# A two-layer attention and convolution chain fed by one weight stream: patch taps moved ahead of the scores, a projection turned later, middle weights as 8 MB loads, constants split

## What is computed

```
fl = _ln(xf, pn_g, pn_b)                       # 64 patches x 1024
pw = _attn(fl, Wqk_p, PDH)                     # Wqk_p 1024 x 2048
pv = _heads(fl @ Wv_p)                         # Wv_p  1024 x 1024
pf = einsum(pw, pv) + _dwconv(pv, conv_p_w, conv_p_b, PPW)
pf = _merge(pf) @ Wout_p                       # Wout_p 1024 x 1024
ww = _attn(_ln(pl, pln_g, pln_b), Wqk_w, WDH)  # Wqk_w 1024 x 2048
diag_scaled, nds = split of ww at its diagonal
wv = _heads(_ln(xw, wn_g, wn_b) @ Wv_w)        # Wv_w   16384 x 1024 (64 MB)
wf = einsum(nds, wv) + _dwconv(wv, conv_w_w, conv_w_b, WN)
out = x + einsum(diag_scaled, _heads(pf)) + _merge(wf) @ Wout_w   # Wout_w 1024 x 16384 (64 MB)
```

## Time and profile before

| | |
|---|---|
| median of 3 runs | 754.56 us (754.07 to 754.59) |
| the profiled execution's own time | 753.38 us |
| its span, first to last instruction | 751.6 us |
| PE busy | 452.6 us, 60% of the span |
| DVE busy | 91.8 us, 12% |
| ACT, POOL busy | 38.0 us, 8.8 us |
| bytes read from device memory | 320.10 million, 427 GB/s over the span |
| mean granted clock of PE | 0.787 of full speed |

### The profile page before, as it was taken

One profiled execution on the slowest core, in us unless ns is written; L12 is line 12 of the kernel. 1 busy time (PEld: TensorE's weight loads), 2 busy tenths in 40 slices (PEclk: granted clock), 3 DMA queues, 4 the chain that ended last, 5 costly groups with the idle time before them and its releaser, 6 DMA issues.

```text
span 751.6 us, 6984 instructions
## 1 busy us (share of the span) xinstructions
PE 452.6 (60%) x3076; PEld 145.0 (19%) x3076; DVE 91.8 (12%) x254; ACT 38.0 (5%) x79; POOL 8.8 (1%) x19
## 2 busy tenths in 40 slices
PE   6599674544546555555587978554454565555547
PEld 5234210000001111111122343100000111111113
DVE  2764400000001000000006062000000010000000
ACT  2111100000000000000001011000000000000000
POOL 2100000000000000000001000000000000000000
PEclk9589886776777777777787999867777777877879
DMA  9999999999999999999999999999999999999996
GB/s 377 432 431 432 451 423 433 429 443 439 419 429 443 443 419 429 436 446 429 420 428 435 425 433 440 416 443 401 446 443 443 398 446 440 443 422 426 443 417 283
DMA packets 7880, 320.81 MB, mean 427 GB/s; under 512 B 905, under 2 KB 1025, under 8 KB 1593
## 3 DMA queue, kind: packets, MB, share of 16 engines
q1 hardware_dynamic: 7488, 320.03, 98.8%
q10 hardware_dynamic: 377, 0.56, 0.2%
HBM read 320.10 MB, written 0.49 MB: 427 GB/s over the span
## 4 chain that ended last, share of the span: by engine, by line
DMA 59%; PE 35%; DVE 5%; ACT 1%; issue 1%; SPq 0%; DVEq 0%; ACTq 0%
DMA ring<-halves 58%; PE bank L489 11%; PE bank L466 10%; PE bank L378 4%; PE bank L387 2%; PE bank L395 1%; PE bank L292 1%; PE bank L444 1%; DVE conv_p L809 1%; DMA cst<-const 1%; PE bank L513 1%; PE bank L358 1%; PE bank L307 1%; DVE ring L681 0%; PE bank L349 0%
## 5 line engine op out<-in xcount | busy, mean ns | idle before, releaser
L466 PE MATMUL bank<-ring,stage 128*4 128x512 f32 x1024 | 142.2, 718 | 130.5 <-DMA ring<-halves 130.5
L489 PE MATMUL bank<-ring,wf_t 128*32 128x512 f32 x1024 | 148.1, 743 | 114.7 <-DMA ring<-halves 114.7
L489 PEld LDWEIGHTS bank<-ring,wf_t 128*32 128x32 f32 x1024 | 36.1, 133 | 215.0 <-DMA ring<-halves 117.7
L466 PEld LDWEIGHTS bank<-ring,stage 128*4 128x4 f32 x1024 | 27.3, 97 | 245.1 <-DMA ring<-halves 143.6
L292 PE MATMUL bank<-cst,area 128*128 128x128 f32 (+1 forms) x234 | 33.0, 286 | 15.5 <-ACT area L616 11.8
L884 DVE TENSOR_TENSOR image<-bank,image 128x32 f32 (+1 forms) x30 | 5.1, 193 | 275.6 <-PE bank L292 275.6
L292 PEld LDWEIGHTS bank<-cst,area 128*128 128x128 f32 (+1 forms) x234 | 28.1, 191 | 35.5 <-ACT area L616 25.4
L858 DVE COPY wv_t<-bank 128x32 f32<-128x32 f32 x2 | 0.4, 192 | 278.3 <-PE bank L292 278.3
L616 ACT COPY area<-bank 128x512 f32<-128x512 f32 x15 | 8.8, 586 | 279.6 <-PE bank L489 279.6
L378 PE MATMUL bank<-extra,area 128*64 128x512 f32 x64 | 17.4, 704 | 1.9 <-DVE area L765 1.9
L444 PE MATMUL bank<-extra,area 128*64 128x512 f32 x64 | 18.4, 741 | 0.0
(11 more groups left out here) (195 smaller groups left out, 205.0 us busy)
## 6 DMA issues: line engine op xcount, KB each, us to landing
ring<-quarters SPq DMA_DIRECT2D x8, 4096.0 KB, 32.3
ring<-halves SPq DMA_DIRECT2D x5, 4096.0 KB, 21.9
extra<-quarters SPq DMA_DIRECT2D x4, 4096.0 KB, 17.2
ring<-halves SPq DMA_DIRECT2D x1, 2048.0 KB, 26.8
ring<-halves SPq DMA_DIRECT2D x2, 1024.0 KB, 29.5
ring<-images SPq DMA_DIRECT2D x1, 512.0 KB, 4.4
ring<-halves SPq DMA_DIRECT2D x29, 29.1
cst<-const SPq DMA_DIRECT2D x1, 461.0 KB, 5.6
```

The source lines that it names most:

```text
L466: m = mm(bank[0][32 * j:32 * j + 4, :], stage[:, k // 8, at:at + 4], w[:, j], start=False, stop=False)
L489: m = mm(bank[6 + g][32 * j:32 * j + 32, :], wf_t[:, h, :], w[:, j], start=(h == 0 and onto is None), stop=(h == GROUP - 1))
```

## The change

Four things are edited.

1. **Order on DVE and PE in the middle of a layer.** The nine patch taps are put in a function `conv_taps(lo, hi)`. Taps 0 to 2 now stand ahead of the wait for the scores, tap 3 inside the softmax, between the subtraction and the wait for the exponential (`meanwhile`), taps 4 to 8 behind it. The copy `wqkt_copied` moves ahead of the packing of the taps.
2. **The projection's turn.** PE's four turns of the scaled `Wout_p` product move from ahead of `Wv_w` to behind it; DVE's four additions to the image move behind `wf_ready`.
3. **Loads.** Slots 4 to 19 of a layer come as two loads of 8 MB instead of four of 4 MB, and PE waits for each as a whole. In the first layer the second of them waits for `image_turned`. The 4 MB ends (`ends`) stay.
4. **Constants.** The identity and the ones are built on POOL. The rest of the table is three loads: the blurs (128 x 256) ahead of the weights, and `const` (128 x 122) and `const_low` (32 x 288) behind the first 4 MB, with the three small loads that ACT issued before, now on SP.

```diff
             sp.dma_start(l0_in[:, :, :], images).then_inc(images_landed, 16)
-            sp.dma_start(cst[:, :], const).then_inc(const_landed, 16)
+            sp.dma_start(cst[:, 0:C_WIDE], blurs).then_inc(blurs_landed, 16)
+            def load_end(L, n):
+                sp.dma_start(extra[:, :], ends[2 * L + n]).then_inc(extra_landed, 16)
+            def load_small():
+                sp.dma_start(area[0][:, :], window_gains).then_inc(gains_landed, 16)
+                sp.dma_start(area[1][0:2 * N_SMALL, 0:P], small).then_inc(small_landed, 16)
+                sp.dma_start(cst[:, C_WIDE:C_LOW], const).then_inc(const_landed, 16)
+                sp.dma_start(cst[0:LOW, C_LOW:], const_low).then_inc(const_landed, 16)
+                sp.dma_start(l2[:, :], l2w).then_inc(l2_landed, 16)
...
             for L in range(2):
-                load_quarter(L, 0)
-                for j in range(1, N_QUARTERS - 1):
-                    if L:
-                        sp.wait_ge(slots_used, used(L, -HALF if j < 3 else 0))
-                    elif j == N_QUARTERS - 2:
-                        sp.wait_ge(image_turned, 1)
-                    load_quarter(L, j)
+                load_end(L, 0)
+                if L == 0:
+                    load_small()
+                if L:
+                    sp.wait_ge(slots_used, used(L, -HALF))
+                load_half(L, -1, 0)
+                if L:
+                    sp.wait_ge(slots_used, used(L, 0))
+                else:
+                    sp.wait_ge(image_turned, 1)
+                load_half(L, -1, 1)
                 sp.wait_ge(slots_used, used(L, QUARTER))
-                load_quarter(L, N_QUARTERS - 1)
+                load_end(L, 1)
...
+            def first_there(L, s):
+                if s in (0, S_VW - QUARTER):
+                    pe.wait_ge(extra_landed, 16 * (2 * L + (2 if s else 1)))
+                elif s in (QUARTER, QUARTER + HALF):
+                    half_there(L, None, s // HALF)
...
-                pe.wait_ge(outp_scaled, L + 1)
-                for s8 in range(4):
-                    m = turn(bank[5][:, s8 * P:s8 * P + P], area[5][:, s8 * P:s8 * P + P])
-                m.then_inc(outp_turned, 1)
...
                 mm(bank[0][:, :], zeros[:, :], area[9][:, :], start=False, stop=True).then_inc(wv_ready, 1)
+                pe.wait_ge(outp_scaled, L + 1)
+                for s8 in range(4):
+                    m = turn(bank[5][:, s8 * P:s8 * P + P], area[5][:, s8 * P:s8 * P + P])
+                m.then_inc(outp_turned, 1)
...
-            act.dma_start(area[0][:, :], window_gains).then_inc(gains_landed, 16)
-            act.dma_start(area[1][0:2 * N_SMALL, 0:P], small).then_inc(small_landed, 16)
-            act.dma_start(l2[:, :], l2w).then_inc(l2_landed, 16)
...
+            g.memset(ones, 1.0).then_inc(ident_built, 1)
+            pool.wait_ge(ident_built, 1)
+            g.affine_select(ident, ones, [[1, P]], ALU.is_equal, 0.0, base=0, channel_multiplier=-1).then_inc(ident_built, 1)
...
+                conv_taps(0, 3)
                 dve.wait_ge(scores_ready, L + 1)
...
-                softmax(L, s4, [soft[:, n, :] for n in range(3)], sub_ready, exp_ready, [P, 4, TOK]).then_inc(probs_ready, 1)
+                softmax(L, s4, [soft[:, n, :] for n in range(3)], sub_ready, exp_ready, [P, 4, TOK], lambda: conv_taps(3, 4)).then_inc(probs_ready, 1)
+
+                conv_taps(4, 9)
+                dve.wait_ge(wqk_turned, L + 1)
+                for n in range(2):
+                    m = v.tensor_copy(wqk_t[:, n, :].rearrange("p (j h w) -> p j h w", j=2, w=4),
+                                      bank[7][:, :].rearrange("p (h j w) -> p j h w", j=4, w=32)[:, 2 * n:2 * n + 2, :, 0:4])
+                m.then_inc(wqkt_copied, 1)
```

More of the change, by code:

```diff
@@ L105, in constants, with build @@
     return c
-def build(nc, images, const, window_gains, small, l2w, quarters, halves, out, windows_last):
+def build(nc, images, blurs, const, const_low, window_gains, small, l2w, ends, halves, out, windows_last):
     with ExitStack() as ctx:
@@ L875, in _ @@
                                 conv_w[:, :, :].rearrange("p (h y) x -> p h y x", y=3)[:, :, 0:2, 0:2], ALU.add).then_inc(wf_ready, 1)
+                dve.wait_ge(outp_turned, L + 1)
+                part = bank[5][:, :].rearrange("p (s f y w n) -> p f w y n s", s=4, f=2, y=8, w=2)
+                rows = pixels.rearrange("p (y n f) (w s) -> p f w y n s", n=4, f=2, s=4)
+                for f in range(2):
+                    for wx in range(2):
+                        m = v.tensor_tensor(rows[:, f, wx], part[:, f, wx], rows[:, f, wx], ALU.add)
+                    m.then_inc(group_added, 1)
+                dve.wait_ge(group_added, added(L))
                 def add_group(i, g):
@@ L932 @@
         smalls += [v[k].reshape(P, 9).T for k in ("conv_p_w", "conv_w_w")]
-        first += [in_tiles(arr(f"{n}_{k}"), QUARTER * SLOT // arr(f"{n}_{k}").shape[1]) for k in ("Wqk_p", "Wv_p", "Wqk_w", "Wout_p")]
+        slots = np.concatenate([in_tiles(arr(f"{n}_{k}"), SLOT // arr(f"{n}_{k}").shape[1]) for k in ("Wqk_p", "Wv_p", "Wqk_w", "Wout_p")])
+        first += [slots[a:a + QUARTER].transpose(1, 0, 2).reshape(1, P, -1) for a in (0, S_VW - QUARTER)]
+        rest += [slots[a:a + HALF].transpose(1, 0, 2).reshape(1, P, -1) for a in (QUARTER, QUARTER + HALF)]
         rest += [in_tiles(arr(f"{n}_Wv_w"), HALF * SLOT // PD)]
@@ L937 @@
         rest += [in_tiles(out_w[:, at:at + SLOT], HALF) for at in range(0, WD, SLOT)]
-    quarters, halves = dram("quarters", np.concatenate(first)), dram("halves", np.concatenate(rest))
+    ends, halves = dram("ends", np.concatenate(first)), dram("halves", np.concatenate(rest))
     l2w = np.concatenate([arr(f"L2_conv_{k}").transpose(1, 2, 3, 0).reshape(C, 9 * C) for k in ("w1", "w2")]
@@ L941 @@
     images = dram("images", np.concatenate([arr("x")[0], arr("L0_conv_style")[0]], 1).transpose(1, 0, 2))
[L942 removed]
+    table = constants()
+    blurs, const, const_low = dram("blurs", table[:, :C_WIDE]), dram("const", table[:, C_WIDE:C_LOW]), dram("const_low", table[:LOW, C_LOW:])
+    l2 = dram("l2w", l2w)
     window_gains, small = dram("window_gains", np.concatenate(gains, 1)), dram("small", np.concatenate(smalls))
@@ L947 @@
     windows_last = nc.dram_tensor("windows_last", (P, WIN * C), F32, kind="ExternalOutput").ap()
-    build(nc, images, const, window_gains, small, l2, quarters, halves, out, windows_last)
+    build(nc, images, blurs, const, const_low, window_gains, small, l2, ends, halves, out, windows_last)
     r = run_bass_kernel_spmd(nc, [arrays], core_ids=[0]).results[0]
```

92 lines of the change are left out of this document (40 added, 52 removed).

## The result

The changed kernel takes 752.58 us (median of 11 runs, 752.04 to 752.87), the one before on the same chip 754.56 (753.38 to 755.98). The ratio is 0.9969 with a 95% interval of 0.9961 to 0.9976, so it is faster by 0.3%, 1.8 to 2.9 us. The forecast was 753.4 in a range of 751.8 to 755.0, with 0.56 for no change within 0.2%, 0.40 for faster and 0.04 for slower. The time lies in the range, 0.8 us under the forecast; what came is the case with 0.40, not the likeliest.

A forecast was written before the change was run, and what follows sets the result against it. The prediction took the weight stream on the main DMA queue to bound the kernel. Order 0.4, loads 0.3 and constants 0.43 summed to 1.1 us off the 754.56 median, giving 753.4 us, range 751.8 to 755.0.

The forecast's parts named there:

- What bounds the kernel: Whole kernel: the main queue's weight stream fills 98.8% of the engines' span; edits count by shortening, advancing or filling it.
- the tail: From the landing at 726.76 us to the span's end: 24.8 us, left alone by the change, moving with the stream.
- Order in the middle: Second layer ahead of `Wv_w`: PE 5.0 us earlier, load issued near 466.4 instead of 471.45; worth 0.4 us.
- the hole: Weight stream at 470 to 475 us, second layer: 315 GB/s, worth 0.28 us by landings, 1.36 by bytes.
- The whole hole: Rival near 470 us: the hole is worth all its bytes, 2.7 us with other upper bounds, 751.9; chance 0.21.
- Constants: Stream's start: 241,664 bytes saved less the overhead of 160 more packets, net 0.43 us, bounds 0.24 and 0.56.
- Loads: Middle weights: eight 4 MB loads become four of 8 MB; fewer load boundaries give 0.3 us, between 0 and 0.75.
- The sum: Whole kernel: 0.4 (order) + 0.3 (loads) + 0.43 (constants) = 1.1 us gained.
- Kept lateness: Rival, loads behind 475 us: without the hole, packets delay later landings; slower by 0.1 to 1.3 us, near 755.3; chance 0.10.
- the 19.5 that would have shown it: Sign of the forecast being wrong: a landing gap over 19.5 us behind 475 us, meaning kept lateness.
- the 19.35 that I named: Sign of the forecast being right, second layer: landings 19.35 us apart from the first.

The follow-up runs named there:

- loads_only: Kernel before with only middle weights as two 8 MB loads: 754.90 us, 1.0002; its three groups: first layer's last 64 records, first 32 of `Wqk_p`, `Wout_p`.
- order_only: Kernel before with only the DVE and PE order changed (taps ahead of the scores, projection turned behind `Wv_w`): 752.70 us, 0.9981.
- taps_only: Kernel before with only the taps ahead of the scores and the window copy ahead of the packing: 753.02 us, 0.9975.
- turn_only: Kernel before with only the projection's turn and additions moved behind `Wv_w`: 753.02 us, 0.9976.
- before_late: Kernel before with four extra products of zeros on PE ahead of `Wv_w` in the second layer: 757.83 us, 1.0042.
- consts_only: Kernel before with only constants split, identity and ones built on POOL, small loads behind the first 4 MB: 754.57 us, 0.9998.
- after_no_order: Changed kernel with the old order on DVE and PE, so 8 MB loads and split constants only: 753.81 us, 0.9986 to before.
- tail_warm: Changed kernel with eight extra products of zeros on PE ahead of its last group but one: 751.62 us, 0.9964 to before.
- before_mid_warm: Kernel before with three extra products of zeros in PE's waits of the second layer's normalisation: 754.33 us, 0.9993.
- quarters_warm: Changed kernel with 4 MB quarters and eight extra products of zeros ahead of PE's last group but one: 752.05 us, 0.9962 to before.

## Why the prediction was right and wrong

**What bounds the kernel.** Right, but for the tail. The landings follow the weight stream, and PE, at 60%, costs only where it makes a load late, and behind the last whole half.

**Order in the middle.** The mechanism was right: the taps fit (0.45 us of wait left of 2.93), the moved work is hidden, the issue came forward by 6.8 us, 5.4 of them by the order, and the hole closed. (Of the 0.4 us over the forecast 5.0, some 0.3 is a slip: the window copy stands on PE's way before and after, so its 0.28 us take nothing from the window scores that leave it.) The term was mis-sized. I took 0.4 us, because PE's landings in the profile of before lay 19.63 us apart. That execution stood at the very edge. Over fourteen profiled executions the gap is 19.34 to 19.50 wherever the issue is at most 94.6 us behind the first layer's last landing; beyond about 95 us it grows about one for one: 19.63 at 95.2, 20.68 at 96.0, 21.7 and 22.0 at 97.3, 22.9 at 98.4. Counted back from the landing of the load ahead, nothing is lost with the issue 3.9 us before it, 0.28 us with 3.2, 1.33 with 2.4, and 3.58 with 0.2: the edge lies some 3.5 us ahead of that landing. The old order, where nothing else speeds PE up, lands on that slope, in four profiled executions from its foot to 2.6 us up, by the clock that PE is granted in the three groups named under loads_only; the profile that I priced it from, 1.18 us under the median of its own runs, was near the foot. That 1.18 us I noted and did not use. What the edits are worth on average is order_only's 1.4 to 1.9 us, taps_only's and turn_only's 1.7 to 1.9. So the 753.4 missed mainly by this term: 0.4 us stood where the runs show 1.4 to 1.9.

**The whole hole as a rival.** Its time, 751.9, was nearer to the result than its 0.21 allowed, but its reason was wrong: the missing bytes of one execution (1.36 us) were not what the landings lost in that execution. It was other executions that lost more. Why a landing loses less than the missing bytes the prediction had right: in before_late the last 64 KB packet of the load ahead starts in 472.00 to 472.25, most engines having nothing left, and at 434/16 = 27.1 GB/s it runs to 474.4 or later (an estimate), just ahead of the landing at 474.96.

**Constants.** 0.43 forecast; the first landing moved 0.53 us in consts_only, and over the quarter kernels from 105.32 (six executions) to 104.87 (three), 0.45. Right.

**Loads.** 0.3 forecast; some 0.4 us by the landings, not confirmed in the times. Together with the constants 0.7 to 1.0 (after_no_order): right in size, a little low.

**The tail.** That the change leaves the 24.8 us alone, so that they move with the stream, was wrong by 0.6 us in the profiled pair: the last group but one took 9.35 us and 10.01. It differs from execution to execution with the granted clock. Over the twelve without extra products ahead of it it took 8.62 to 10.01 us, so the changed kernel's was the longest of all, and nothing shows that the change made it so. tail_warm shows that the clock costs 2.9 us of PE in that execution, of which 0.4 to 1.0 is time.

**The sum in the profiled pair.** That the last landing moved by 1.22 us, near the sum of 1.1, is partly luck. By the first layer's last landing it is 0.61, up to the second layer's first 0.23 more, and the hole adds only 0.17 of its 0.4; 0.19 come from a gap behind 629 us that no term names.

**Kept lateness.** It was not seen. In after, the largest gap between landings behind 475 is the first, 19.46, under the 19.5 that would have shown it, though not the 19.35 that I named. Before has one of 19.56 (629.76 to 649.32), where after has 19.37 (628.76 to 648.13). Other executions have up to 19.70 there (consts_only), with either order; its cause is open.

## What to carry to other kernels

In a kernel bound by a weight stream, work on the compute engines costs nothing until it makes a load late, and then it costs its full length (the work behind the last landings apart): find for each load how long before the queue's end it is issued, and treat that as a margin with a spread, not as a number. A hole of 0.3 us in one profile was worth 1.4 to 1.9 us in the medians and ratios, with the margin near zero. What moves such a margin can be the granted clock of a few matmul groups, and one such group made faster need not help: in before_mid_warm a later one gave back most of it. Hold the profiled execution against the spread of the runs first; where it lies at one end, the term that varies is not the one the profile shows. Once a margin is wide enough, a second edit that widens it gives nothing.

## What was not expected of the hardware

A run of products with no use, put into a wait for a load, kept PE's granted clock at the higher level (1.00, the 2.4 GHz level) through the landing in tail_warm: 64 records in 7.07 us, where twelve executions without them took 8.62 to 10.01. The products ended 0.84 us before the landing. With 2.18 us of idle between, in quarters_warm, it was 8.77, no gain that can be told. Each is one execution. In the normalisation three such products held 1.00 where 0.69 had been granted, and `Wout_p`, from 450.51 on, took 9.44 us instead of 8.40.
